# Projection and Gram product in a recommendation tower: from 128-row matmuls to pairs of 64-row matmuls, with the projection's bias copied into its banks ahead

## What is computed

```
x = layer_norm(dense @ Wd.T, gd, bd)                    # 512 samples x 128
y = layer_norm(einsum('bnd,ed->bne', e, Ws), gs, bs)    # e: 26 gathered embedding rows of 64 per sample
y = einsum('bne,pn->bep', y, Wsi)                       # the 26 rows mixed to 32
y = swapaxes(layer_norm(y, gsi, bsi), 1, 2)             # normed over the 32
T = concatenate([x[:, None, :], y], axis=1)             # 33 rows of 128
Z = einsum('bnd,bmd->bnm', T, T)                        # the lower triangle is used
z = layer_norm(Zflat @ Wl.T, gl, bl)[:384]
h = relu(concat(z, dense) @ W_top1 + b_top1)
h = relu(h @ W_top2 + b_top2)
out = h @ W_top3
```

## Time and profile before

| | us |
|---|---|
| runs shown | 194.11, 193.77, 193.14 |
| median | 193.77 |
| the profiled execution | 194.12 |
| its span, first to last instruction | 192.2 |
| busy: PE, PEld, DVE, ACT, POOL | 148.4, 96.9, 99.7, 89.6, 101.6 |

### The profile page before, as it was taken

The page is one execution under the profiler, slowest core; times in us unless marked ns, Lnnn a source line. Parts: engine busy times, 40 slices in busy tenths (PEclk is TensorE's granted clock), DMA queues, the critical chain, the costliest instruction groups (busy, mean ns, idle before and its releaser), DMA issues.

```text
span 192.2 us, 4178 instructions
## 1 busy us (share of the span) xinstructions
PE 148.4 (77%) x1644; PEld 96.9 (50%) x1644; DVE 99.7 (52%) x192; ACT 89.6 (47%) x225; POOL 101.6 (53%) x113
## 2 busy tenths in 40 slices
PE   0496496958767976488869867798695889989995
PEld 0343444534444643354457646455565566446674
DVE  2390946684916882838073847361838456541001
ACT  3613043744512566755545436436744546641251
POOL 4777364757874487676375774776757720000000
PEclk9999669999979999969999999999999999999999
DMA  5813131416311015431011155111011640025000
GB/s 143 272 30 76 34 110 26 127 26 211 116 28 22 10 27 129 72 55 27 9 21 20 30 139 80 31 34 20 20 24 27 156 66 3 3 65 106 6 3 0
DMA packets 20260, 11.58 MB, mean 60 GB/s; under 512 B 12945, under 2 KB 17681, under 8 KB 20242
## 3 DMA queue, kind: packets, MB, share of 16 engines
q1 hardware_dynamic: 16226, 7.83, 15.2%
q0 software_dynamic: 3328, 3.41, 10.0%
q10 hardware_dynamic: 688, 0.08, 0.3%
HBM read 9.15 MB, written 2.16 MB: 59 GB/s over the span
## 4 chain that ended last, share of the span: by engine, by line
PE 40%; POOL 20%; DMA 13%; DVE 11%; issue 9%; ACT 5%; SPq 1%; POOLq 1%; DVEq 0%; ACTq 0%
POOL e_rows L373 20%; DMA e_rows<-table_dram,rows_sb 7%; PE mix_ps L440 7%; PE o_ps L488 5%; PE quad_ps L451 5%; PE proj_ps L474 4%; DMA dense_sb<-dense_t_dram 3%; DVE e_unit L910 3%; DVE e_prod L882 3%; DVE var_n L885 3%; PE dots_ps L465 3%; PE turn_ps L432 2%; PE o_ps L403 2%; PE dots_ps L396 2%; PE o_turn_ps L403 2%
## 5 line engine op out<-in xcount | busy, mean ns | idle before, releaser
L373 POOL DMA_INDIRECT e_rows<-table_dram,rows_sb x104 | 100.7, 968 | 53.1 <-issue 27.7
L440 PE MATMUL mix_ps<-mixw_sb,e_unit 128*128 128x192 f32 (+4 forms) x128 | 23.0, 325 | 17.0 <-DVE e_unit L910 17.0
L440 PEld LDWEIGHTS mix_ps<-mixw_sb,e_unit 128*128 128x128 f32 x128 | 20.0, 199 | 25.6 <-DVE e_unit L910 25.6
L882 DVE TENSOR_TENSOR e_prod<-quad_ps,e_rows 128x384 f32<-128x384 f32 (+1 forms) x16 | 9.5, 591 | 45.2 <-PE quad_ps L451 45.2
L474 PE MATMUL proj_ps<-f_sb,proj_w 128*128 128x512 f32 x60 | 32.5, 625 | 0.0
L873 DVE TENSOR_REDUCE var_p<-y_sq 128x16 f32<-128x512 f32 x32 | 20.5, 677 | 1.6 <-ACT y_sq L665 1.6
L451 PEld LDWEIGHTS quad_ps<-gram,e_cols 128*128 128x128 f32 x104 | 14.5, 206 | 12.2 <-ACT e_cols L673 11.2
L680 ACT COPY f_sb<-mix_ps 64x512 f32<-64x512 f32 x32 | 18.5, 578 | 4.5 <-PE mix_ps L440 4.1
L665 ACT ACTIVATE y_sq<-proj_ps 128x512 f32<-128x512 f32 x30 | 17.7, 589 | 5.9 <-PE proj_ps L474 5.7
L432 PE MATMUL turn_ps<-small_sb,e_rows 128*128 128x128 f32 x52 | 9.7, 302 | 13.9 <-DMA e_rows<-table_dram,rows_sb 13.8
L897 DVE TENSOR_TENSOR feats<-proj_ps,rstd_p 128x512 f32<-128x512 f32 x30 | 19.3, 686 | 0.6
(11 more groups left out here) (142 smaller groups left out, 172.8 us busy)
## 6 DMA issues: line engine op xcount, KB each, us to landing
z_dram<-z_mine SPq DMA_DIRECT2D x4, 512.0 KB, 3.2
e_rows<-table_dram,rows_sb POOLq DMA_INDIRECT x104, 2.5
w_sb<-w_dram SPq DMA_DIRECT2D x2, 512.0 KB, 6.6
wl_sb<-wl_dram SPq DMA_DIRECT2D x2, 512.0 KB, 3.4
w_sb<-w_dram SPq DMA_DIRECT2D x1, 768.0 KB, 4.2
dense_sb<-dense_t_dram SPq DMA_DIRECT2D x1, 512.0 KB, 5.8
wl_sb<-wl_dram SPq DMA_DIRECT2D x1, 256.0 KB, 2.7
z_pairs<-z_dram SPq DMA_DIRECT2D x4, 64.0 KB, 2.0
```

The source lines that it names most:

```text
L373: pool.indirect_dma_start(out=e_rows[:, chunk, t, D * ab:D * (ab + 1)], out_offset=None, in_=table, in_offset=bass.IndirectOffsetOnAxis(ap ...
L440: mm = pe.matmul(mix_ps[:, PR * at:PR * (at + number)], e_unit[:, t, :], mixw_sb[:, t, lo:lo + number, :].rearrange("k b p -> k (b p)"), s ...
```

## The change

The projection of a slot is done as two matmuls that use 64 rows of the array each: half a with rows 0 to 63 of `f_sb` and `proj_w`, half b with rows 64 to 127 of both. `f_sb` is therefore saved by one copy of 128 rows in place of two of 64, `proj_w` holds the weights twice, and the bias has no row any more: ACT copies it (`y_seed`, 128 x 512) into both banks of `proj_ps` ahead of each projection (`seed`), which then adds to the banks' content. For slot 0 two matmuls with the identity put it there. `seed(i)` waits for both instructions of `norm_p(i-1)` and stands in ACT's list behind the tower's pieces and ahead of `save_z(i-2)`. Both halves are projected ahead of `quad`. In the last round they come behind `dots(last - 1)`, and the last slot uses `proj_ps` like the others.

The Gram product is done as two matmuls per tile, each with 64 rows and 64 columns of output: half a into `quad_ps`, half b into `turn_ps`. DVE's product L882 becomes two instructions of half the size. `turn(i)` also waits for the product of slot i-1.

```diff
+        quad_half_ps = [quad_ps, turn_ps]
-        proj_last_ps = [turn_ps[:], quad_ps[:]]
...
-        f_sb = sb("f_sb", [P, 2, 2, 512])
+        f_sb = sb("f_sb", [P, 2, 512])
+        y_seed = sb("y_seed", [P, 512])
...
-        gram = sb("gram", [P, P])
+        gram = sb("gram", [P, D])
...
-            pool.memset(gram[:], 0.0).then_inc(consts, 1)
-            pool.memset(proj_w[:], 0.0).then_inc(consts, 1)
...
                 wait(pe, cols_ready, s)
+                wait(pe, prod_done, s)
...
                 for t in range(nt):
-                    mm = pe.matmul(quad_ps[:, P * t:P * (t + 1)], e_cols[:, q % 2, P * t:P * (t + 1)], gram[:],
-                                   start=True, stop=True)
+                    for ab in range(2):
+                        half = slice(D * ab, D * (ab + 1))
+                        mm = pe.matmul(quad_half_ps[ab][:, D * t:D * (t + 1)], e_cols[half, q % 2, P * t:P * (t + 1)],
+                                       gram[half, :], start=True, stop=True)
...
-            def project(s, ab):
+            def project(s):
+
                 _, q = place(s)
-                if s < SLOTS - 1:
-                    wait(pe, y_ready, 2 * s - 1 + ab)
-                pe.wait_ge(f_ready, 2 * s + ab + 1)
-                pe.matmul(proj_of(s, ab), proj_w[:], f_sb[:, q % 2, ab, :], start=True,
-                          stop=True).then_inc(projected, 1)
+                pe.wait_ge(f_ready, s + 1)
+                if s == 0:
+                    pe.wait_ge(prep_act, 7)
+                    for ab in range(2):
+                        pe.matmul(proj_ps[:, ab, :], eye_sb, y_seed[:], start=True, stop=True)
+                wait(pe, seeded, 2 * s)
+                for ab in range(2):
+                    half = slice(D * ab, D * (ab + 1))
+                    pe.matmul(proj_ps[:, ab, :], proj_w[half, :], f_sb[half, q % 2, :], start=False, stop=True,
+                              skip_group_check=True).then_inc(projected, 1)
...
                 turn(i)
                 if i >= 1:
-                    project(i - 1, 0)
+                    project(i - 1)
                 quad(i)
-                if i >= 1:
-                    project(i - 1, 1)
...
             linear(CHUNKS - 2, range(1, 2))
-            project(last, 0)
-            project(last, 1)
             dots(last - 1)
+            project(last)
             linear(CHUNKS - 2, range(2, KZ))
...
                 wait(act, projected, 2 * s - 2)
+                act.copy(f_sb[:, q % 2, :], mix_ps[:]).then_inc(f_ready, 1)
+
+            def seed(s):
+
                 for ab in range(2):
-                    act.copy(f_sb[0:D, q % 2, ab, :], mix_ps[D * ab:D * (ab + 1), :]).then_inc(f_ready, 1)
+                    act.wait_ge(y_ready, 2 * (s - 1) + ab + 1)
+                    act.copy(proj_ps[:, ab, :], y_seed[:]).then_inc(seeded, 1)
...
                 if i == 10:
                     relu_2_early(0)
+                if i >= 1:
+                    seed(i)
                 if 2 <= i < SLOTS - 2:
                     save_z(i - 2)
...
             save_f(last)
+            seed(last)
             square(last, 0)
...
-                dve.tensor_tensor(e_prod[:, 0:2 * nt, :].rearrange("p a d -> p (a d)"), quad_ps[:, 0:P * nt],
-                                  e_rows[:, chunk, t0:t0 + nt, :].rearrange("p t d -> p (t d)"), ALU.mult).then_inc(prod_done, 1)
+                for ab in range(2):
+                    last_prod = dve.tensor_tensor(e_prod[:, 0:2 * nt, :].rearrange("p (t a) d -> p a t d", a=2)[:, ab, :, :],
+                                           quad_half_ps[ab][:, 0:D * nt].rearrange("p (t d) -> p t d", d=D),
+                                           e_rows[:, chunk, t0:t0 + nt, D * ab:D * (ab + 1)], ALU.mult)
+                last_prod.then_inc(prod_done, 1)
```

More of the change, by code:

```diff
@@ L110 @@
 PACK = {}
-for _name, _width in (("eye", P), ("ws", EW), ("wsi", PR), ("gs", 1), ("gd", 1), ("bd", 1),
+for _name, _width in (("eye", P), ("ws", EW), ("wsi", PR), ("gs", 1), ("bs", 1), ("gd", 1), ("bd", 1),
                       ("gl", USED // P), ("bl", USED // P), ("b1", H1 // P), ("b2", H2 // P), ("w3", H2 // P)):
@@ L281, in o_turned_to @@
             return o_turn_ps[:, P * j:P * (j + 1)]
-        def proj_of(s, ab):
-            return proj_last_ps[ab] if s == SLOTS - 1 else proj_ps[:, ab, :]
         def samples(chunk):
@@ L437, in mix @@
                 pe.wait_ge(unit_ready, s + 1)
-                wait(pe, f_ready, 2 * s)
+                wait(pe, f_ready, s)
                 for n, (t, lo, at, number) in enumerate(mix_parts(q)):
@@ L601, in _ @@
             turn(last)
-            project(last - 1, 0)
+            project(last - 1)
             quad(last)
-            project(last - 1, 1)
             dots(last - 2)
@@ L634, in _ @@
             act.wait_ge(prep_pe, 1)
-            for half in range(2):
-                for ab in range(2):
-                    last = act.copy(f_sb[D:P, half, ab, :].rearrange("p (b q) -> p b q", q=PR),
-                                    quad_ps[D:P, 0:PR].unsqueeze(1).to_broadcast([P - D, QB, PR]))
-            last.then_inc(prep_act, 1)
+            act.activation(y_seed[:].rearrange("p (b q) -> p b q", q=PR), quad_ps[:, 0:PR].unsqueeze(1).to_broadcast([P, QB, PR]),
+                           ACT.Copy, scale=bs_sb[:, 0:1]).then_inc(prep_act, 1)
             act.wait_ge(prep_pe, 2)
             act.copy(ws_rows[:], turn_ps[:, 0:D].unsqueeze(1).to_broadcast([P, 2, D])).then_inc(prep_act, 1)
-            act.activation(ws_grows[:], turn_ps[:, 0:D], ACT.Copy, scale=gs_sb[:, 0:1]).then_inc(prep_act, 1)
+            act.activation(ws_grows[:], turn_ps[:, 0:D].unsqueeze(1).to_broadcast([P, 2, D]), ACT.Copy,
+                           scale=gs_sb[:, 0:1]).then_inc(prep_act, 1)
             act.wait_ge(prep_pe, 3)
-            act.copy(gram[0:D, 0:D], mix_ps[0:D, 0:D])
-            act.copy(gram[D:P, D:P], mix_ps[D:P, 0:D]).then_inc(prep_act, 1)
+            act.copy(gram[:], mix_ps[:, 0:D]).then_inc(prep_act, 1)
             act.wait_ge(prep_pe, 4)
-            act.copy(proj_w[D:D + 1, :], ws_sb[D:D + 1, :])
-            act.copy(proj_w[0:D, :], o_turn_ps[0:D, 0:EW]).then_inc(prep_act, 1)
+            act.copy(proj_w[:], o_turn_ps[:, 0:EW]).then_inc(prep_act, 1)
             act.wait_ge(prep_pe, 5)
@@ L665, in square @@
                 act.activation(y_sq[:, QB * ab:QB * (ab + 1), :].rearrange("p b q -> p (b q)"),
-                               proj_of(s, ab), ACT.Square).then_inc(sq_ready, 1)
+                               proj_ps[:, ab, :], ACT.Square).then_inc(sq_ready, 1)
             def save_cols(s):
@@ L897, in norm_p @@
                     dve.tensor_tensor(feats[:, q % 2, QB * ab:QB * (ab + 1), 2:PR + 2],
-                                      proj_of(s, ab).rearrange("p (b q) -> p b q", q=PR),
+                                      proj_ps[:, ab, :].rearrange("p (b q) -> p b q", q=PR),
                                       rstd_p[:, QB * ab:QB * (ab + 1)].unsqueeze(2).to_broadcast(wide),
@@ L1037 @@
     put("eye", np.eye(P, dtype=np.float32))
-    put("ws", np.concatenate([a["L0_rec_Ws"].T, a["L0_rec_bs"][None]]))
+    put("ws", a["L0_rec_Ws"].T)
     put("wsi", a["L0_rec_Wsi"].T)
     put("gs", columns(a["L0_rec_gs"]))
+    put("bs", columns(a["L0_rec_bs"]))
     put("gd", columns(a["L0_rec_gd"]))
```

14 lines of the change are left out of this document (7 added, 7 removed).

## The result

| | before | changed |
|---|---|---|
| median of the runs, us | 193.94 | 219.71 |
| lowest to highest, us | 193.14 to 196.0 | 217.93 to 223.46 |
| profiled execution, its span, us | 194.12, 192.2 | 217.93, 215.5 |
| mean granted clock | 0.964 | 0.850 |

The account below looks back on a forecast made before the run. It took the chain of waits, not PE's busy time, as the bound: two rounds cost the gathers and one round's work. Terms 1.7 + 1.7 + 1.6 + 0.6 + 0.8 + 2.4 + 0.8 = 9.6 gave 203.4 us, range 198 to 213.5.

Parts of the forecast that it names:

- What the change takes off PE: Both projections ahead of quad: 0.86 us on the path before and after; PE time saved in the gap priced at nothing.
- A colder clock: Rival: less PE work, longer gaps; one or two more slow rounds at +1.5 us, 205 to 207; within the forecast's 0.60.
- Pairs overlap: Projections: the two halves of the array work at once, so both projections of a slot take 0.86 us, not 1.72.
- `quad` at 0.67: Gram product as 12 MATMULs of 64 columns, paired: 0.67 us, unchanged, the middle of 0.34 and 1.3.
- Step 1: Ten path rounds: change to 64-row use 0.1 us and DVE's product in two 0.07, 0.17 per round, 1.7 in all.
- Step 2: Round 1: two identity matmuls of 512 columns fill proj_ps ahead of the first projection, 1.72 us on the path.
- Step 3: Round 2: the seed stands behind save_dense(2) in ACT's list and the projection waits for it, +1.6 us.
- Steps 4 to 6: Seeds behind norm_p (round 5, +0.6 us), gain_wl (rounds 6 and 7, +0.8 together), scale_o (rounds 8 and 12, +1.2 each).
- Step 7: The end: the last projections wait for norm_p(14) and the seed and reach ACT later, +0.8 us to the output.
- gaps in which the clock falls in many rounds: Last of the listed signs that would show the forecast wrong; no size given.

Follow-up runs that it names:

- The narrowed projection: Kernel before with the second projection of each slot but the last cut to 32 of 512 columns; 199.51 us, ratio 1.036.
- the fill: Changed kernel plus one overwritten full-row matmul of 512 columns ahead of each mix from slot 1 on; 203.77 us, then 202.88 us in another series.
- The filled change without seeds: Changed kernel with the full-row matmul ahead of mix, without ACT's bias copies and round 1's identity matmuls; 195.11 us, ratio 1.011.

## Why the prediction failed, step by step

**The step that failed is the price of the idle gap.** Under "What the change takes off PE" the prediction says that what is saved "is PE time in the gap, which becomes idle. I price this at nothing", and under its rivals it gives "A colder clock" one or two rounds at 1.5 us. The idle time itself is free, as it said; the clock behind it is not. Measured: 51 us more at half clock, worth by the estimate above 0.39 x 51 = 20 us. The narrowed projection isolates one part (6 us for an emptier gap), the fill reverses most of it (16 us back by the medians, at least 10), and 20 of the 51 us come with the seeds, whose waits the prediction counted without a clock. The evidence was in the row that the rival rested on, round 7 at the lower level, after gaps of 1.5 us ahead of `mix(6)` and 2.1 ahead of `turn(7)`. Ahead of `mix`, the kernel before has a gap of 2.8 us in round 0 and none over 1.6 after it; the changed kernel has 2.0 to 2.5 in rounds 1, 2, 6, 8 and 12, and 1.4 to 1.7 in five more. The rival was counted per round that happened to be late, instead of per round that loses its cover. No single gap tells whether the clock will fall: before, gaps of 1.5 to 1.6 us in rounds 1, 2, 8 and 12 were not followed by a fall.

Both parts together: 6 to 8 us on the path and 20 of clock, 26 to 28, against 219.71 - 193.94 = 25.8 and 218.78 - 191.79 = 27.0 measured. The change without its Gram part does not fit this account, as said above.

**Pairs overlap: right.** 0.97 us from the projections' start to `quad`: 0.86 of work and 0.1 more, which lies between the first two MATMULs and the second two (0.53 us where one takes 0.43). Each projection group's first two MATMULs, one of each half, start at the same time within 0.01 us. Weight loads of 64 rows took 0.19 us (median), as those of 128 rows did before. The weighed rule of the Trainium skill ("TensorE: Matmul & The Clock Gate", Part 3, "What overlaps and what doesn't"), from which the prediction worked out 1.29 us, is not what these rows show, while that Part's "The mechanism", which has row tiles start some nanoseconds apart, agrees with them.

**`quad` at 0.67: right.** From the second on, the pairs start 0.11 us apart (116.86, 116.97 and so on), as the full ones did; the first is 0.05 ahead.

**Step 1, 1.7 us: near.** The traces show its pieces. The change of use ahead of the projection takes its 0.1 us, and the 0.1 more of the last paragraph but one, which the step had not counted, comes on top: from the last MATMUL of `turn` to `quad` it is 1.165 us where it was 0.97. From `quad` to DVE's product it is 0.04 less, and from the product to the sum 0.66 in place of 0.59. That is 0.22 per round where 0.17 was taken. The filled change without seeds is 195.11 - 191.79 = 3.3 us above before, of which 0.39 x 3.4 = 1.3 is clock: 2.0 left. The ratio's interval, 1.001 to 1.021, leaves this open by some 2 us either way.

**Step 2, 1.72: right.** Comparing the filled change with and without seeds, the lead over from `turn(1)` to `turn(2)` grew by 1.64 us (25.98 to 36.12 against 26.72 to 35.22).

**Step 3, 1.6: a little high.** `turn(2)` to `turn(3)` grew by 1.3 us in that pair; the wait itself was 1.54 [the row of round 2 above].

**Steps 4 to 6, 0.6 + 0.8 + 2.4: sizes off.** In the same pair round 5 grew by 0.1 instead of 0.6, rounds 8 and 12 by 0.5 and 0.9 instead of 1.2 each, rounds 6 and 7 by 4.4 instead of 0.8. The last is mostly clock: by its clock records that pair's kernels spent 13.6 us of these two rounds at the lower level with seeds and 3.4 without, and 0.39 x 10.2 = 4.0. The waits for the seeds were found in rounds 2, 7, 8 and 12, as forecast, but not in round 5. In the filled change, whose rounds are shorter, there is one of 0.55 us in round 5, and others in rounds 3 (1.43), 6, 11 and 15; the prediction has nothing for round 3 and calls 11 and 15 covered.

**Step 7, 0.8: the sum near, its cause not the seed alone.** From `turn(15)` to the last instruction the changed kernel takes 215.5 - 179.47 = 36.0 us, the kernel before 192.2 - 157.44 = 34.8: 1.2 with round 15's own 0.17. But the two kernels without seeds take 36.0 (with the fill) and 36.4 (without it), so most of it comes with the rest of the last round, where the last projections stand behind `dots` and wait for `norm_p(14)`.

**What it asked to see.** PE's busy time was to fall by 15 us and rose by 11; `turn(15)` was to start 8 to 9 us later and started 22 later. Both are mostly the clock (with the fill `turn(15)` starts 7 us later, at 164.72), which it had named last, as "gaps in which the clock falls in many rounds".

## What to carry to other kernels

Work that TensorE does while it would wait anyway is not free to remove: it may be what holds the clock. Before taking matmuls out of a gap, list the rounds that lose their cover, compare their gaps with those of rounds in which the clock fell, and price each by the rows at the lower level. That gives a rival with its price, not a rule. Where such gaps can't be closed with useful work, try a discarded full-row matmul in them; it is cheap to test and was worth 10 to 16 us here.

## What was not expected of the hardware

- 15 discarded matmuls, 0.86 us each, made the kernel 7% faster (218.78 to 202.88 us, medians), and 15 such matmuls in eleven places took the kernel before to a mean clock of 1.000 and 0.8% off its time.
- A discarded matmul on 64 rows, of the same length on PE, did less than one on 128: 34 to 41 us at half clock against 24 to 28, and 6.6 us of time lost.
- An us at the lower level cost 0.39 us in the changed kernel. Taking 14 of them out of the kernel before gave 1.9 us, 0.13 each, with the fills' own cost in it.
- The change from 128-row to 64-row use took 0.1 us: 0.20 from the last full-row start to the first 64-row start, where 0.11 is the spacing.
- On one chip PE stood still for 13 to 21 us of each profiled execution with nothing to wait for, and the kernel before took 201.17 us in place of 192 to 194.
